# Whole tiles first in both expert layers, four row buffers in the first, and no closing drain of GpSimd

## The chip, the cores and the metric

The kernel runs on one core of one Trainium2 chip. The metric is the time of one execution on the device in microseconds (us); lower is better. One execution was also taken by the hardware profiler, and the rows below come from that one.

## The reference, cut to what matters

Two layers, each of a conditioning block and an expert block with two experts per token, on 2048 tokens of 512 numbers:

```python
x = x + L0_ffn(L0_cond(x))      # attention over a paged cache, then 8 sparse weight sets, 2 per token
x = x + L1_ffn(L1_cond(x))      # linear with a low-rank adapter, then 8 experts, 2 per token
# L0_ffn: logits = clip(xt @ gate_w.T); top 2, softmax; per expert a sparse delta added to W
# L1_ffn: probs = softmax(x @ gate_w); top 2
h = gelu(x @ fc1_w[e] + fc1_b[e], approximate=False)
y = h @ fc2_w[e] + fc2_b[e];    out = sum over the 2 chosen e of combine[t, e] * y
```

With 2 experts per token, 4096 rows go through each expert layer. The router's choices are known only while the kernel runs. Worked out from the reference with its inputs, the eight experts get 542, 416, 510, 556, 504, 526, 508 and 534 rows in the first layer and 542, 526, 490, 492, 520, 543, 510 and 473 in the second.

## The kernel before, in words

**Routing.** Every token's row (512 numbers and four of bookkeeping, `DX` = 516) is sent by GpSimd with an indirect DMA (`send`) to each of its two experts' regions in a DRAM tensor, `rows`. The semaphores `xs_sc` (first layer) and `x2_sc` (second) count these sends. VectorE keeps a running end of each region (`run`); when the last token is placed, `ends()` signals `r_end`, and `tiles()` makes the list of tiles: for tile t of 39 (`NTILE`) the expert (`ex_i`) and the first row (`row_i`) of 128 rows, in order of experts, each expert's partly filled tile right behind its full ones. It signals `r_ok`. 39 is the most that 4096 rows in 8 regions can need; tiles past the last used one read a region of zeros.

**Zeros.** Because a partly filled tile reads past its region's end, 128 rows of zeros are written behind each of the eight ends (`zero_ends`: for each expert a register load of the end and a DMA of 258 KB), four by the SP queue and four by the ACT queue, as soon as `r_end` is there. The semaphore `zrows` counts them. SP waits for `zrows` and for all sends before it fetches the first tile.

**First expert layer.** Tiles go in pairs through two slots. SP fetches the rows into `xs_in[s]` (two buffers); the next fetch into a buffer waits until TensorE has turned it (`l_tx`) and VectorE has copied the four bookkeeping columns (`l_mt`, in `take_meta`). TensorE turns four 128x128 blocks, ScalarE copies them to `xs_t`, TensorE multiplies with the expert's weights (`m_w`), VectorE scales out of PSUM into `y_sb[s]` (line 1801), and GpSimd adds the rows to `acc0` or `acc1` in DRAM by an indirect DMA (line 653). VectorE may write `y_sb[s]` again only when that DMA has landed (`l_st`). Behind each of the first eight pairs ScalarE issues a load of 1 MB of the second layer's weights (`load_fc`). Before the first tile TensorE also waits for `m_done` = 16, the signal of VectorE's last addition to the weights (line 1556), which stands in VectorE's order behind `tiles()`.

**Second expert layer.** The same with `xs_in[s]`, but VectorE copies the turned rows (`turned1`, line 1867), ScalarE copies the expert's fc1 matrix (`weights`, line 1211) and does the gelu, and the rows are added to `out`. A pair is 80 matmuls or so on TensorE.

**The end.** The five engines' programs stand in a block. At its end each engine drains (line 66), and all of them meet. GpSimd comes there last, after it has waited for the last addition into `out`.

Of the kernel before, what the change touches and what calls it, by code (L numbers as in the profile page):

```python
# [9 lines left out]
I32 = mybir.dt.int32  # L10
# [4 lines left out]
P = 128  # L15
# [21 lines left out]
PAIRS = (NTILE + 1) // 2  # L37
BOTH, LAST = (0, 1), tuple(range(NTILE - 2 * (PAIRS - 1)))
# [25 lines left out]
def program(nc, d):  # L64
    ctx = ExitStack()
    with ctx:
# [33 lines left out]
        tile_ii = words(R3, 7700, [NTILE], I32)  # L100
# [37 lines left out]
        xs_in = [words(R3, DX * s, [DX]) for s in range(2)]  # L138
        xs_t = [words(R3, 1032 + 512 * s, [KC, P]) for s in range(2)]
        h_t = [words(R3, 2056 + 512 * s, [KC, P]) for s in range(2)]  # L140
        y_sb = [words(R3, 3080 + 512 * s, [D]) for s in range(2)]
        fc1_s = [words(R3, 4104 + 2048 * s, [KC, D]) for s in range(2)]
# [102 lines left out]
        ntf = [sb(f"ntf{i}", [P, NE]) for i in range(4)]  # L245
        slot_f = sb("slot_f", [P, 2, 2])
        slot_i = sb("slot_i", [P, 2, NT], I32)
        ex_c = words(masks, 0, [NTILE, NE])
        ex_f = sb("ex_f", [P, NTILE])
# [3 lines left out]
        tile_io = sb("tile_io", [P, NTILE])  # L253
# [15 lines left out]
        for name in ("rope_d gain_d p0_dma table_d imp_d mask_d atoms_d w_kv w_q raw_dma consts zero_ok rope_in rope_r idx_ok idx_n eaw_in imp_s eaw_ok mark_in mark_ok "  # L269
                     "delta wgt_ok eqa cell_ok pre_w pre_c b1_p zdone r_end zrows mscat bk bc e_in e_lg e_row "  # L270
                     "s_dot s_mx s_exp s_sc s_pt s_pe s_pv s_ot m_done att_w kv_mm kv_sq kv_nr rst step p1r p1o o_p1 o_k o_kc q_ss q_nw q_rp xq "
                     "r_sel r_slot r_ok l_f l_ex l_mt k_mt r_l r_lexp acc_z xs_sc x2_sc w5 w1_ok b1_d b2_d fc1_d fc2_d c_rt c_rtc").split():
            S[name] = sem(name)
        S2 = {}
        for name in ("mstage kvd kvc "
                     "l_in l_tx l_xt l_mm l_ye l_st k_in k_tx k_xt k_w k_m1 k_hg k_m2 k_ye k_yb k_st "
                     "c_in c_x1 c_tx c_xt c_xa c_xe c_h c_x2 c_g c_st").split():
            S2[name] = sem2(name)
        S4 = {name: [sem(f"{name}_{i}") for i in range(4)] for name in ("x_in", "p1k")}
# [26 lines left out]
        block = ctx.enter_context(nc.Block())  # L306
# [10 lines left out]
        def _(sp):  # L317
# [104 lines left out]
            def expert_io(layer, sent, load, read, meta_read):  # L422

                def fetch(row, s):
                    sp.dma_start(xs_in[s], rows_d[bass.ds(row, P), :]).then_inc(load[s], 16)

                def rows_of(t, slots=BOTH):
                    return [sp.value_load(row_i[0:1, bass.ds(t + s, 1)], min_val=0, max_val=ROWS - P) for s in slots]

                def following(i, slots):  # L430
                    rows = rows_of(2 * i + 2, slots)
                    sp.wait_ge(meta_read, i + 1)
                    for s in slots:
                        sp.wait_ge(read[s], i + 1)
                        fetch(rows[s], s)

                sp.wait_ge(S["r_ok"], layer)
                rows = rows_of(0)
                sp.wait_ge(S["zrows"], 16 * NE * layer)
                sp.wait_ge(sent, 32 * NT)  # L440
                for s in range(2):
                    fetch(rows[s], s)
                yield
                with sp.Fori(0, PAIRS - 2) as i:
                    following(i, BOTH)
                following(PAIRS - 2, LAST)
# [31 lines left out]
            io = expert_io(2, S["x2_sc"], S2["k_in"], S2["k_tx"], S["k_mt"])  # L478
            next(io)
            sp.dma_start(b2_bc, d["b2"].partition_broadcast(P)).then_inc(S["b2_d"], 16)  # L480
            for _ in io:
                pass
# [3 lines left out]
        def _(po):  # L486
            po.iota(iot[:, 0:32], [[1, 32]], base=0, channel_multiplier=0)
            po.iota(iot[:, 32:33], [[0, 1]], base=0, channel_multiplier=1)
            po.iota(tile_ii, [[1, NTILE]], base=0, channel_multiplier=0)
# [188 lines left out]
        def _(pe):  # L678
# [205 lines left out]
            def turn_x(load, done, turned, i, s):  # L884
                pe.wait_ge(load[s], 16 * i + 16)
                wait(pe, done[s], i)
                turn4(ps[:, s, :], xs_in[s]).then_inc(turned[s], 1)

            def layer0(i, now, after):
                es = [pe.value_load(ex_i[0:1, bass.ds(2 * i + s, 1)], min_val=0, max_val=NE - 1) for s in now]  # L890
                for s in now:
                    pe.wait_ge(S2["l_xt"][s], i + 1)
                    wait(pe, S2["l_ye"][s], i)
                    chunks(ps[:, 2 + s, :], lambda k: xs_t[s][:, k, :], lambda k: m_w[:, k, es[s], :]
                           ).then_inc(S2["l_mm"][s], 1)
                    if s in after:
                        turn_x(S2["l_in"], S2["l_xt"], S2["l_tx"], i + 1, s)

            for s in range(2):
                turn_x(S2["l_in"], S2["l_xt"], S2["l_tx"], 0, s)  # L900
            with pe.Fori(0, PAIRS - 2) as i:
                layer0(i, BOTH, BOTH)
            layer0(PAIRS - 2, BOTH, LAST)
            layer0(PAIRS - 1, LAST, ())

# [51 lines left out]
            def layer1(i, now, after):  # L957
# [9 lines left out]
                for s in after:  # L967
                    turn_x(S2["k_in"], S2["k_xt"], S2["k_tx"], i + 1, s)
# [6 lines left out]
            for s in range(2):  # L975
                turn_x(S2["k_in"], S2["k_xt"], S2["k_tx"], 0, s)
            with pe.Fori(0, PAIRS - 2) as i:
                layer1(i, BOTH, BOTH)
# [5 lines left out]
        def _(ac):  # L984
# [143 lines left out]
            zero_ends(ac, 1, range(NE // 2, NE))  # L1128
# [69 lines left out]
            zero_ends(ac, 2, range(NE // 2, NE))  # L1198
# [26 lines left out]
            with ac.Fori(0, PAIRS - 2) as i:  # L1225
                gelu(i, BOTH, BOTH)
# [5 lines left out]
        def _(ve):  # L1232
# [410 lines left out]
            def tiles():  # L1643

                def step(ins):
                    ve.drain()
                    return ins
                ve.drain()
                step(TT(ntf[0][:], run[:], region0[:], ALU.subtract))
                step(TS(ntf[0][:], ntf[0][:], float(P - 1), None, ALU.add))  # L1650
                step(CP(nti[:], ntf[0][:]))
                step(TS(nti[:], nti[:], 7, None, ALU.arith_shift_right))
                CP(ntf[2][:], nti[:])
                step(CP(ntf[0][:], nti[:]))
                u, v = ntf[0], ntf[1]
                for sh in (1, 2, 4):
                    TT(v[:, sh:], u[:, sh:], u[:, :NE - sh], ALU.add)
                    step(CP(v[:, :sh], u[:, :sh]))
                    u, v = v, u
                TS(ntf[3][:], ntf[2][:], -float(P), float(REGION), ALU.mult, ALU.add)  # L1660
                ve.drain()
                step(TT(ex_c[:], u[:].unsqueeze(1).broadcast_to([P, NTILE, NE]),
                        tile_io[:].unsqueeze(2).broadcast_to([P, NTILE, NE]), ALU.is_le))
                step(red(ex_f[:], ex_c[:, :, 0:NE - 1], ALU.add))
                CP(ex_i[:], ex_f[:])
                TS(ex_r[:, 0:NTILE], ex_f[:], -1.0, float(NE), ALU.mult, ALU.add)
                step(TT(ex_c[:], ex_c[:], ntf[3][:].unsqueeze(1).broadcast_to([P, NTILE, NE]), ALU.mult))
                step(red(ex_f[:], ex_c[:], ALU.add))
                step(ve.scalar_tensor_tensor(ex_f[:], tile_io[:], float(P), ex_f[:], ALU.mult, ALU.add))
                CP(row_i[:], ex_f[:])  # L1670
                ve.drain().then_inc(S["r_ok"], 1)
                CP(run[:], region0[:])
# [91 lines left out]
            tiles()  # L1764
# [4 lines left out]
            def take_meta(i, load, slots, taken):  # L1769

                for s in slots:
                    ve.wait_ge(load[s], 16 * i + 16)
                    CP(meta[:, s, :], xs_in[s][:, D:DX])
                ve.drain().then_inc(taken, 1)

# [7 lines left out]
            def layer0(i, slots, after):  # L1783
# [4 lines left out]
                if after:  # L1788
                    take_meta(i + 1, S2["l_in"], after, S["l_mt"])
# [13 lines left out]
            take_meta(0, S2["l_in"], BOTH, S["l_mt"])  # L1803
            mark(x2_rows, 0, NT)
            with ve.Fori(0, PAIRS - 2) as i:
                layer0(i, BOTH, BOTH)
            layer0(PAIRS - 2, BOTH, LAST)
            layer0(PAIRS - 1, LAST, ())
# [50 lines left out]
            tiles()  # L1859
            for s in range(2):  # L1860
                ve.wait_ge(S2["c_st"][s], 16 * (NT // 2))
# [7 lines left out]
            def layer1(i, now, after):  # L1869
# [9 lines left out]
                if after:  # L1879
                    take_meta(i + 1, S2["k_in"], after, S["k_mt"])  # L1880
# [12 lines left out]
            take_meta(0, S2["k_in"], BOTH, S["k_mt"])  # L1893
# [66 lines left out]
```

## Time and profile before

| | |
|---|---|
| time, median of 3 runs | 1059.96 us (1058.91, 1059.96, 1066.42) |
| time of the profiled execution | 1056.38 us |
| its span, first to last instruction | 1054.2 us |
| mean granted clock of TensorE | 0.952 |

The span is what the rows below divide up. The profiled execution took 2.2 us more than its span; that rest lies outside of all instructions shown. The profiled execution was 3.6 us (0.34%) below the median.

### The profile page before, as it was taken

The page shows a single profiled execution, that of the slowest core. Times are in us where ns is not written, and L with a number is a line of the kernel's source. Part 1 is how long each engine was busy: PE and PEld are TensorE (multiplying, and loading weights), DVE is VectorE, ACT ScalarE, POOL GpSimd, SP SyncE. Part 2 cuts the span into 40 slices and gives each one's busy share as a digit, 9 for nine tenths or more (in the row PEclk, how much of TensorE's full clock was granted, in tenths as well). Part 3 has the DMA queues.
Part 4 walks back from the last instruction along what each step waited for, and adds up shares of the span by engine and source line. Part 5 has one row for each costly group of instructions (what it writes and reads, how often), then busy time and mean ns, then how long its engine had stood idle before and what let it go on. Part 6 is the DMA issues. An engine that isn't in the chain of part 4 may idle for free.

```text
span 1054.2 us, 18329 instructions
## 1 busy us (share of the span) xinstructions
PE 932.6 (88%) x4690; PEld 604.2 (57%) x4691; DVE 547.0 (52%) x2190; ACT 416.5 (40%) x1273; POOL 364.7 (35%) x475
## 2 busy tenths in 40 slices
PE   6999998989998888379899969994799999999994
PEld 2457555555455444234344438884577777777772
DVE  4777687776678987623334424555233333333331
ACT  3654465555655555011111112221354455444540
POOL 3575244666663250313334321324022121222121
PEclk9996999999999999779999989998799999999998
DMA  7854923353355361578777747974442334323430
GB/s 249 271 221 138 343 63 102 82 146 94 72 162 163 105 222 60 183 234 218 204 161 137 131 110 244 387 278 167 175 80 46 68 68 78 60 61 66 77 47 0
DMA packets 76455, 152.11 MB, mean 144 GB/s; under 512 B 16743, under 2 KB 22007, under 8 KB 74736
## 3 DMA queue, kind: packets, MB, share of 16 engines
q1 hardware_dynamic: 40240, 87.27, 25.0%
q0 software_dynamic: 24832, 42.71, 20.1%
q10 hardware_dynamic: 11328, 21.51, 6.2%
q8 instruction: 20, 0.33, 0.1%
q14 instruction: 35, 0.29, 0.1%
HBM read 94.05 MB, written 69.00 MB: 155 GB/s over the span
## 4 chain that ended last, share of the span: by engine, by line
PE 63%; DVE 13%; DMA 9%; issue 7%; ACT 2%; DVEq 2%; SPq 1%; POOL 1%; ACTq 0%; POOLq 0%
PE ps L681 52%; DMA acc<-R,tok_i 5%; PE ps L687 4%; DVE R L1538 2%; PE ps L751 2%; DVE R L1556 2%; DVE R L1527 2%; ACT R L1042 1%; PE ps L739 1%; DMA R<-rows 1%; DMA rows<-zrow 1%; DMA R<-m_buf 1%; PE ps L732 1%; DMA R<-in_x_t 1%; PE ps L783 1%
## 5 line engine op out<-in xcount | busy, mean ns | idle before, releaser
L681 PE MATMUL ps<-R 128*128 128x128 f32 (+4 forms) x2768 | 685.3, 404 | 15.7 <-DMA R<-in_x_t 10.4
L681 PEld LDWEIGHTS ps<-R 128*128 128x128 f32 x2768 | 420.4, 194 | 240.2 <-issue 217.6
L653 POOL DMA_INDIRECT out_x<-R,tok_i x39 | 60.5, 1552 | 249.0 <-DVEq L1892 160.8
L687 PE MATMUL ps<-ident,R 128*128 128x128 f32 x440 | 67.6, 286 | 55.3 <-DMA R<-rows 39.0
L580 POOL DMA_INDIRECT rows<-R,slot_i x64 | 65.7, 1026 | 137.1 <-ACT lg L1174 73.2
L1058 ACT ACTIVATE R<-R,nmx 128x384 f32<-128x384 f32 x128 | 78.4, 622 | 77.7 <-DVE nmx L1527 77.7
L687 PEld LDWEIGHTS ps<-ident,R 128*128 128x128 f32 x440 | 53.8, 147 | 89.1 <-issue 75.8
L653 POOL DMA_INDIRECT acc<-R,tok_i x39 | 60.5, 1552 | 117.1 <-DVE R L1801 107.5
L1527 DVE CUSTOM_DVE_ANT_0 R<-ps,R,q_scale 128x384 f32<-128x384 f32 x128 | 73.7, 613 | 30.5 <-issue 30.5
L1219 ACT ACT_TABLE_LOAD x18 | 23.1, 1283 | 145.5 <-PE ps L681 145.5
L739 PE MATMUL ps<-ident,R 128*128 128x128 f32 x384 | 56.5, 283 | 24.5 <-DVE R L1538 13.0
L1887 DVE TENSOR_TENSOR R<-ps,R 128x512 f32<-128x512 f32 x39 | 27.0, 692 | 95.9 <-PE ps L681 95.9
L1211 ACT ACTIVATE R<-R 128x2048 f32 x39 | 75.6, 1940 | 1.4 <-issue 1.4
L739 PEld LDWEIGHTS ps<-ident,R 128*128 128x128 f32 x384 | 42.8, 143 | 49.8 <-DVE R L1538 25.5
L588 POOL DMA_INDIRECT m_buf<-tot,cell_i x32 | 51.4, 1607 | 37.1 <-DMA m_buf<-tot,cell_i 29.8
L1144 ACT ACTIVATE R<-ps 128x512 f32<-128x512 f32 x39 | 23.3, 597 | 95.1 <-PE ps L687 93.1
L732 PE MATMUL ps<-R 64*128 64x384 f32 x256 | 60.0, 548 | 0.9 <-ACT R L1031 0.9
L1064 ACT ACTIVATE R<-ps 128x384 f32<-128x384 f32 x128 | 56.7, 508 | 6.2 <-PE ps L739 6.1
L1867 DVE COPY R<-ps 128x512 f32<-128x512 f32 x39 | 25.3, 687 | 53.3 <-PE ps L687 53.1
L1219 ACT ACTIVATE R<-ps,inv_f 128x128 f32<-128x128 f32 x156 | 44.8, 381 | 18.4 <-PE ps L681 18.2
L1538 DVE TENSOR_SCALAR R<-R,rsum 128x384 f32<-128x384 f32 x128 | 49.2, 427 | 5.0
L751 PE MATMUL ps<-R 128*64 128x256 f32 x384 | 49.3, 392 | 0.0
(282 smaller groups left out, 919.2 us busy)
## 6 DMA issues: line engine op xcount, KB each, us to landing
R<-rows SPq DMA_DIRECT2D x78, 258.0 KB, 3.4
R<-in_fc ACTq DMA_DIRECT2D x16, 1024.0 KB, 6.6
m_buf<-R SPq DMA_DIRECT2D x8, 1024.0 KB, 8.2
R<-m_buf SPq DMA_DIRECT2D x16, 512.0 KB, 4.7
R<-acc SPq DMA_DIRECT2D x32, 256.0 KB, 5.9
R<-in_x_t SPq DMA_DIRECT2D x4, 1024.0 KB, 8.8
R<-in_x_t SPq DMA_DIRECT2D x8, 512.0 KB, 3.4
new_kv<-R SPq DMA_DIRECT2D x16, 256.0 KB, 3.1
```

The costliest lines, as they stand in the source:

```text
L580: po.indirect_dma_start(out=rows_d, out_offset=bass.IndirectOffsetOnAxis(ap=slot_i[:, c, t:t + 1], axis=0), in_=rows[:, t, :], in_offset=N ...
L653: po.indirect_dma_start(out=sums[s], out_offset=bass.IndirectOffsetOnAxis(ap=tok_i[:, s:s + 1], axis=0), in_=y_sb[s], in_offset=None, boun ...
L681: m = pe.matmul(out, lhs(k), rhs(k), start=(k == 0 and first), stop=(k == KC - 1 and last))
L687: m = pe.transpose(out[:, k * P:(k + 1) * P], src[:, k * P:(k + 1) * P], ident[:])
L732: pe.matmul(ps[:, 2 + u % 4, 0:KW], q_t[s][base:base + 64, jj, qt * P:(qt + 1) * P], k_t[s][base:base + 64, p, qt * P:qt * P + KW], start= ...
L739: m = pe.transpose(ps[:, 6 + u % 2, c * P:(c + 1) * P], prob[u % 4][:, c * P:(c + 1) * P], ident[:])
L751: n = pe.matmul(ps[HD * x:HD * (x + 1), 1, KC // 2 * P * (m % 2):KC // 2 * P * (m % 2 + 1)].rearrange("p (i q) -> p i q", q=P), kv[s][:, q ...
L1058: ac.activation(prob[u % 4], msk_s[u % 4], ACT.Exp, bias=nmx[:, u:u + 1], scale=-1.0, accum_out=sums[:, u:u + 1]).then_inc(S["s_exp"], 1)
L1211: ac.activation(fc1_s[s], fc1[:, :, e, :], ACT.Copy).then_inc(S2["k_w"][s], 1)
L1219: g = ac.activation(h_t[s][:, c, :], ps[:, 2 + s, c * P:(c + 1) * P], ACT.Gelu, bias=b1_t[:, e, c:c + 1])
L1527: ve.tensor_tensor_reduce(out=msk_s[u % 4], in0=ps[:, 2 + u % 4, 0:KW], in1=mask[:, u // NH, :], scale=q_scale[:, B % 2, u:u + 1], scalar= ...
L1538: TS(prob[u % 4], prob[u % 4], rsum[:, u % NH:u % NH + 1], None, ALU.mult).then_inc(S["s_sc"], 1)
```

## The change

Seven things are changed.

1. `tiles()` makes the list in two parts. The first 24 tiles (`FULL`) are taken from those whose 128 rows are all taken; 24 of them there are always. It signals `r_ok` behind these. Then it works out the other 15 (`REST`): the whole tiles that are left, then the partly filled ones, then unused ones. Behind these it signals a new semaphore, `q_ok`. In the first layer VectorE's last addition to the weights stands behind both parts.
2. SP fetches the first tiles on `r_ok` and the sends alone, and waits for `zrows` and `q_ok` only before it fetches the tile with index 24. TensorE, and in the second layer ScalarE, wait for `q_ok` at the same place in their loops, which are cut in two there.
3. SP's four writes of zeros follow its first fetches (in the second layer also the load of `b2_bc`, 2 MB).
4. ScalarE's four writes of zeros move: in the first layer behind the second pair's `load_fc`; in the second behind the first two copies of fc1 and a new wait for `x2_sc`.
5. The first layer's rows have four buffers. Four tiles are fetched at the start, and the pair i+2 is fetched when the pair i is turned and its bookkeeping is copied. Its loops do two pairs per turn.
6. Some buffers of `R3` shift by 8 words to make room.
7. The block is opened with `no_gpsimd_drain=True`.

```diff
-        block = ctx.enter_context(nc.Block())
+        block = ctx.enter_context(nc.Block(no_gpsimd_drain=True))
...
+            sp.wait_ge(S["r_ok"], 1)
+            rows = rows_of(0, range(4))
+            sp.wait_ge(S["xs_sc"], 32 * NT)
+            for b in range(4):
+                fetch(rows[b], b, S4["l_in"][b])
             zero_ends(sp, 1, range(NE // 2))
-            for _ in expert_io(1, S["xs_sc"], S2["l_in"], S2["l_tx"], S["l_mt"]):
-                pass
+            with sp.Fori(0, FP // 2 - 1) as h:
+                rows0(2 * h, 0)
+                rows0(2 * h + 1, 2)
+            sp.wait_ge(S["q_ok"], 1)
+            sp.wait_ge(S["zrows"], 16 * NE)
+            with sp.Fori(FP // 2 - 1, PAIRS // 2 - 2) as h:
+                rows0(2 * h, 0)
+                rows0(2 * h + 1, 2)
...
+            sp.wait_ge(S["r_ok"], 2)
+            rows = rows_of(0)
+            sp.wait_ge(S["x2_sc"], 32 * NT)
+            for s in BOTH:
+                fetch(rows[s], s, S2["k_in"][s])
+            sp.dma_start(b2_bc, d["b2"].partition_broadcast(P)).then_inc(S["b2_d"], 16)
             zero_ends(sp, 2, range(NE // 2))
...
-            zero_ends(ac, 1, range(NE // 2, NE))
             ac.wait_ge(S["xs_sc"], 32 * NT)
...
                 load_fc(fc1, fc1_v, i, S["fc1_d"])
+                if i == 1:
+                    zero_ends(ac, 1, range(NE // 2, NE))
...
-            zero_ends(ac, 2, range(NE // 2, NE))
...
             for s in range(2):
                 weights(0, s)
-            with ac.Fori(0, PAIRS - 2) as i:
+            ac.wait_ge(S["x2_sc"], 32 * NT)
+            zero_ends(ac, 2, range(NE // 2, NE))
+            with ac.Fori(0, FP - 1) as i:
+                gelu(i, BOTH, BOTH)
+            ac.wait_ge(S["q_ok"], 2)
+            with ac.Fori(FP - 1, PAIRS - 2) as i:
                 gelu(i, BOTH, BOTH)
```

The second part of the new `tiles(layer)`, in full:

```python
ve.drain().then_inc(S["r_ok"], 1)
CP(seg_end[:, 0:NE], u[:])
step(ve.scalar_tensor_tensor(n_row, n_full, -float(P), n_row, ALU.mult, ALU.add))
step(TS(n_part, n_row, 0.0, None, ALU.is_gt))
u = ends_of(n_part, ntf[0], ntf[1])          # three steps of two instructions
TS(seg_end[:, NE:2 * NE], u[:], seg_end[:, NE - 1:NE], None, ALU.add)
step(ve.scalar_tensor_tensor(n_gap, n_part, -float(P), ntf[3][:], ALU.mult, ALU.add))
CP(seg_gap[:, 0:NE - 1], ntf[3][:, 0:NE - 1])
step(ve.scalar_tensor_tensor(seg_gap[:, NE - 1:NE], n_full[:, 0:1], float(P), ntf[3][:, NE - 1:NE], ALU.mult, ALU.add))
TS(seg_gap[:, NE - 1:NE], seg_gap[:, NE - 1:NE], -float(NE * REGION), None, ALU.add)
ve.scalar_tensor_tensor(seg_gap[:, NE:2 * NE - 1], n_full[:, 1:NE], float(P), n_gap[:, 0:NE - 1], ALU.mult, ALU.add)
CP(seg_gap[:, 2 * NE - 1:2 * NE], n_gap[:, NE - 1:NE])
step(ve.memset(seg_e, 1.0))
ve.memset(seg_e[:, NE - 1:NE], 1.0 - NE)
step(ve.memset(seg_e[:, 2 * NE - 1:2 * NE], 0.0))
...
shape = [P, REST, 2 * NE]
step(TT(c, seg_end.unsqueeze(1).broadcast_to(shape), tile_io[:].unsqueeze(2).broadcast_to(shape), ALU.is_le))
step(TT(w, c, seg_e.unsqueeze(1).broadcast_to(shape), ALU.mult))
step(red(ex_f[:, 0:REST], w, ALU.add))
CP(ex_i[:, FULL:], ex_f[:, 0:REST])
TS(ex_r[:, FULL:NTILE], ex_f[:, 0:REST], -1.0, float(NE), ALU.mult, ALU.add)
step(TT(w, c, seg_gap.unsqueeze(1).broadcast_to(shape), ALU.mult))
step(red(ex_f[:, 0:REST], w, ALU.add))
step(ve.scalar_tensor_tensor(ex_f[:, 0:REST], tile_io[:], float(P), ex_f[:, 0:REST], ALU.mult, ALU.add))
CP(row_i[:, FULL:], ex_f[:, 0:REST])
ve.drain().then_inc(S["q_ok"], 1)
```

## Rows read from the trace of the kernel before

**Rows 1.** The page, its chain that ended last, shares by line.

```profile
PE ps L681 52%; DMA acc<-R,tok_i 5%; PE ps L687 4%; DVE R L1538 2%; PE ps L751 2%; DVE R L1556 2%; DVE R L1527 2%; ACT R L1042 1%; PE ps L739 1%; DMA R<-rows 1%; DMA rows<-zrow 1%; DMA R<-m_buf 1%; PE ps L732 1%; DMA R<-in_x_t 1%; PE ps L783 1%
```

**Rows 2.** Stretches: us, busy PE, PEld, DVE, ACT, POOL, clock, DMA share, GB/s.

```profile
463.00:620.00 157.00, 148.87 (x450) 71.35 (x448) 62.49 (x264) 26.00 (x56) 58.99 (x38) 1.00 0.73 165
...
757.00:1041.00 284.00, 282.58 (x1645) 207.47 (x1643) 92.67 (x319) 128.92 (x206) 58.96 (x38) 1.00 0.34 62
```

**Rows 3.** The last addition: the chain, its landing, and line 66's drain.

```profile
1043.46 1.55 POOL out_x L653
```

```profile
out_x<-R,tok_i POOLq DMA_INDIRECT x1, 2.7
```

```profile
L66 POOLq DRAIN  x1: 7579/7579/7579, 1046.4 to 1046.4; - x1
```

**Rows 4.** The chain into the first expert layer: start, length, what.

```profile
444.81 5.55 DMA rows<-zrow
450.52 2.66 DMA R<-rows
453.32 1.94 PE ps L687 x8
```

**Rows 5.** The chain into the second expert layer.

```profile
741.87 2.54 DMA R<-rows
...
746.49 0.89 issue
747.38 9.71 PE ps L681 x64
```

**Rows 6.** SP's wait for the sends, when it ended in each layer.

```profile
L440 SPq EVENT_SEMAPHORE  x2: 17/17/17, 449.0 to 740.8; - x2
```

**Rows 7.** GpSimd's last sends of both layers, in order of time.

```profile
443.00 0.96 POOL L580 DMA_INDIRECT rows<-R,slot_i  x1 [0.30 <-issue]
...
734.54 0.96 POOL L580 DMA_INDIRECT rows<-R,slot_i  x1 [0.30 <-issue]
```

**Rows 8.** Landing of two sends: that of 728.16 us, that of 734.54 us.

```profile
DMA to landing us min/median/max: 2.7/2.7/2.7
...
DMA to landing us min/median/max: 6.2/6.2/6.2
```

**Rows 9.** VectorE in the old list, in order of time.

```profile
441.79 0.17 DVE L1660 TENSOR_SCALAR ntf<-ntf 128x8 f32<-128x8 f32 x1
442.03 0.48 DVE L1662 TENSOR_TENSOR masks<-ntf,tile_io 128x312 f32<-128x312 f32 x1
```

**Rows 10.** VectorE around the end of the list, in order of time.

```profile
445.05 1.07 DVE L1556 TENSOR_TENSOR R<-R 128x512 f32<-128x512 f32 x1
...
735.56 0.18 DVE L1670 CAST row_i<-ex_f 128x39 int32<-128x39 f32 x1
```

**Rows 11.** SP's register loads of tile rows: count, min/median/max ns.

```profile
L428 SPq TENSOR_LOAD <-row_i x78: 261/268/1024, 445.2 to 997.0; - x78
```

**Rows 12.** ScalarE's queue, its four writes of zeros.

```profile
440.21 4.78 ACTq L313 DMA_DIRECT2D rows<-zrow  x4
```

**Rows 13.** The chain in the first expert layer: two of the additions.

```profile
469.19 7.17 DMA acc<-R,tok_i
...
505.86 8.01 DMA acc<-R,tok_i
```

**Rows 14.** Waits in 466 to 536 us: total, times, longest.

```profile
PE ps L687 <- DMA R<-rows: 5.5, 5, 1.3
...
PE ps L681 <- DVE R L1801: 1.0, 5, 0.2
```

**Rows 15.** Stretches as in group 2.

```profile
466.00:476.00 10.00, 10.00 (x34) 5.04 (x33) 2.99 (x13) 2.00 (x4) 3.17 (x3) 1.00 0.92 216
...
744.00:746.00 2.00, 1.46 (x7) 1.34 (x8) 0.68 (x3) 0.00 (x0) 0.00 (x0) 0.50 1.11 386
...
752.00:754.00 2.00, 2.00 (x18) 2.00 (x18) 0.34 (x2) 0.38 (x1) 0.00 (x0) 0.94 0.05 18
```

More of the change, by code:

```diff
@@ L420, in _ @@
                 fetch_m(m)
[L422 to L446, printed above, removed]
@@ L448, in _, with rows_of, fetch, rows0 @@
-            zero_ends(sp, 1, range(NE // 2))
-            for _ in expert_io(1, S["xs_sc"], S2["l_in"], S2["l_tx"], S["l_mt"]):
-                pass
+            def rows_of(t, slots=BOTH):
+                return [sp.value_load(row_i[0:1, bass.ds(t + s, 1)], min_val=0, max_val=ROWS - P) for s in slots]
+            def fetch(row, b, load):
+                sp.dma_start(xs_in[b], rows_d[bass.ds(row, P), :]).then_inc(load, 16)
+            def rows0(i, b, slots=BOTH):
+                rows = rows_of(2 * i + 4, slots)
+                sp.wait_ge(S["l_mt"], i + 1)
+                for s in slots:
+                    sp.wait_ge(S2["l_tx"][s], i + 1)
+                    fetch(rows[s], b + s, S4["l_in"][b + s])
@@ L476, in _ @@
                 sp.wait_ge(S2["c_tx"][s], NT // 2)
-            zero_ends(sp, 2, range(NE // 2))
[L478 to L482, printed above, removed]
+            sp.wait_ge(S["r_ok"], 2)
+            rows = rows_of(0)
+            sp.wait_ge(S["x2_sc"], 32 * NT)
+            for s in BOTH:
+                fetch(rows[s], s, S2["k_in"][s])
+            sp.dma_start(b2_bc, d["b2"].partition_broadcast(P)).then_inc(S["b2_d"], 16)
+            zero_ends(sp, 2, range(NE // 2))
+            with sp.Fori(0, FP - 1) as i:
+                rows1(i)
+            sp.wait_ge(S["q_ok"], 2)
+            sp.wait_ge(S["zrows"], 32 * NE)
+            with sp.Fori(FP - 1, PAIRS - 2) as i:
+                rows1(i)
+            rows1(PAIRS - 2, LAST)
         @block.gpsimd
@@ L882, in _, with turn_x, turn_x0, turn_x2 @@
             pe.wait_ge(S["m_done"], 16)
-            def turn_x(load, done, turned, i, s):
-                pe.wait_ge(load[s], 16 * i + 16)
+            def turn_x(x, load, landed, done, turned, i, s):
+                pe.wait_ge(load, landed)
                 wait(pe, done[s], i)
-                turn4(ps[:, s, :], xs_in[s]).then_inc(turned[s], 1)
-            def layer0(i, now, after):
+                turn4(ps[:, s, :], x).then_inc(turned[s], 1)
+            def turn_x0(i, h, b, s):
+                turn_x(xs_in[b + s], S4["l_in"][b + s], 16 * h + 16, S2["l_xt"], S2["l_tx"], i, s)
+            def turn_x2(i, s):
+                turn_x(xs_in[s], S2["k_in"][s], 16 * i + 16, S2["k_xt"], S2["k_tx"], i, s)
+            def layer0(h, odd, now, after):
+                i = 2 * h + odd
                 es = [pe.value_load(ex_i[0:1, bass.ds(2 * i + s, 1)], min_val=0, max_val=NE - 1) for s in now]
@@ L967, in layer1 @@
                 for s in after:
[L968 removed]
+                    turn_x2(i + 1, s)
                 for s in now:
@@ L975, in _ @@
             for s in range(2):
-                turn_x(S2["k_in"], S2["k_xt"], S2["k_tx"], 0, s)
-            with pe.Fori(0, PAIRS - 2) as i:
+                turn_x2(0, s)
+            with pe.Fori(0, FP) as i:
+                layer1(i, BOTH, BOTH)
+            pe.wait_ge(S["q_ok"], 2)
+            with pe.Fori(FP, PAIRS - 2) as i:
                 layer1(i, BOTH, BOTH)
@@ L1641, in ends, with tiles @@
                 ve.drain().then_inc(S["r_end"], 1)
-            def tiles():
+            def tiles(layer):
                 def step(ins):
@@ L1652, in tiles @@
+                step(CP(nti[:], n_row))
                 step(TS(nti[:], nti[:], 7, None, ALU.arith_shift_right))
[L1653 to L1660, printed above, removed]
@@ new lines, in tiles @@
+                if layer == 1:
+                    for s in range(2):
+                        ve.wait_ge(S2["c_st"][s], 16 * (NT // 2))
+                c, w = rest_c[layer], rest_m[layer]
+                shape = [P, REST, 2 * NE]
+                step(TT(c, seg_end.unsqueeze(1).broadcast_to(shape), tile_io[:].unsqueeze(2).broadcast_to(shape), ALU.is_le))
+                step(TT(w, c, seg_e.unsqueeze(1).broadcast_to(shape), ALU.mult))
+                step(red(ex_f[:, 0:REST], w, ALU.add))
@@ L1763, in _ @@
             ends()
-            tiles()
+            tiles(0)
             for _ in adds:
@@ L1858, in _ @@
             ends()
-            tiles()
-            for s in range(2):
-                ve.wait_ge(S2["c_st"][s], 16 * (NT // 2))
+            tiles(1)
             def turned1(i, slots):
@@ L1879, in layer1 @@
                 if after:
-                    take_meta(i + 1, S2["k_in"], after, S["k_mt"])
+                    meta1(i + 1, after)
                 if after:
```

112 lines of the change are left out of this document (73 added, 39 removed).

## The prediction

> **What bounds the kernel now.** I read the chain that ended last first. TensorE's matmuls carry half of it [rows 1]; the writes of zeros, the fetches of rows and the additions into `acc` carry 1%, 1% and 5%. The stretches say where TensorE is not full: in the second expert layer it is busy for 282.6 of 284 us, in the first for 148.9 of 157 [rows 2]. So a change to the order of tiles can win at four places only: at the end, at the two entries and in the 8.1 us of gaps inside the first layer.
>
> At the end the last addition is issued at 1043.46 and lands 2.7 us later, at 1046.2 [rows 3]. Then GpSimd drains for 7.58 us, and the kernel ends with it.
>
> At both entries the chain runs through a write of zeros: it lands at 450.36, SP fetches at 450.52, the rows land 2.66 us later, TensorE starts at 453.32 [rows 4]. In the second layer the fetch is at 741.87 and the first matmul of fc1 at 747.38 [rows 5]. The zeros cost twice. They are waited for, and they make the sends slow: a send shortly before them lands in 2.7 us, the last one, in their midst, in 6.2 [rows 8], so that SP has all sends only at 449.0 and 740.8 [rows 6].
>
> Inside the first layer, the chain is one of additions of slot 1: each lands 7.2 to 8.0 us after its issue [rows 13], each beside a load of 1 MB. The five waits of TensorE for rows (5.5 us) are followed by five short waits for VectorE's scaling (1.0 us) [rows 14]. Both end together: VectorE could scale only when the addition before had landed.
>
> **The closing drain.** One instruction of 7.58 us goes [rows 3]; nothing else is at work then, and what is late next is the meeting of the engines at 1046.4 plus some 0.2 us. Ends: 0 (the time comes again elsewhere) and 7.6. I take **-7.6**, since GpSimd's own wait has already seen the last landing, and nothing that is computed hangs on the drain.
>
> **Entry to the second layer.** The sends: the last is issued at 734.54 [rows 7]; without zeros beside it it lands in 2.7 us [rows 8], at 737.25. The list: the old one was ready at 735.75 [rows 10]. Its new first part has one small step and one small copy less (0.24 + 0.08 us), and four large instructions shrink from 312 elements or so to 192. By the slope of the two rows [rows 9], (0.48 - 0.17) / 304 = 1.02 ns an element, that is 4 x 0.12. It is ready 0.8 us earlier, at 734.95. Two register loads of 0.27 to 1.0 us [rows 11], each with some 0.3 us of checks behind it (an estimate), are done by 737.5. The fetch goes at about 737.4 in place of 741.87, the rows land at 739.95 and are turned by 742.05; with 0.89 us of TensorE's own loads [rows 5] fc1 could start at 742.95.
>
> VectorE must by then have copied the turned rows, and it has got the second part of the list. Small steps stand 0.24 us apart [rows 9]: 11 of them (first scalar-tensor step, comparison, three of `ends_of`, two gaps, two memsets, the row number, the last cast) are 2.6 us; 5 large steps of 240 elements, 0.41 + 0.07 each, 2.4; a dozen instructions without a drain between, about 0.08 each, 1.0. Sum 6.0 us, to 741.0. Then bookkeeping and the first copy: about 742.3. That is 0.65 us ahead of TensorE, so it is hidden, just. **-4.4 us** (747.38 to 742.95). Ends: -2.2, if the clock (below) or a long second part takes half; -4.6.
>
> ScalarE's zeros now stand behind its first fc1 copies; its queue needs 4.8 us for them [rows 12], from about 740.2 to 745, and the first gelu is due only when the first tile's fc1 is through, after 748. SP's zeros stand ahead of the second pair's fetch, as they stood ahead of the first; that fetch leaves at about 745.5 and has until TensorE has done 64 matmuls, 9.7 us [rows 5], at 752.6. With the 2 MB of `b2_bc`, 4.6 MB are moved in the 15 us between: 310 GB/s, less than the 386 that 744 to 746 us reach [rows 15]. I cost both at 0; without that cover it would be up to 2 us.
>
> **Entry to the first layer.** The last send is issued at 443.00 [rows 7], lands at 445.7. SP has four register loads now, so it fetches between 446.4 and 449 and has rows at 449.1 to 451.7. But TensorE also waits for VectorE's last addition to the weights. It was at 445.05 and took 1.07 us [rows 10], under cover of the zeros. Now the second part stands ahead: 444.2 + 6.0 + 0.1 + 1.1 = 451.4. That cover is gone, and the addition becomes the gate: TensorE starts at 451.5 in place of 453.32, **-1.8 us**. Ends: -3 (rows as gate), 0 (a longer second part).
>
> **Inside the first layer.** Four buffers take away the five waits for rows. Yet the matmul behind each waits for VectorE's scaling, and that for a landed addition; only the 0.2 us each by which the scaling was waited for after the turn come free, and only the last stays won: **-0.2 us**. End: -8.1, all gaps of group 2.
>
> ScalarE's four zeros, 1.03 MB, now follow its second load on the same queue. They meet the addition of 469.19, which landed in 7.17 us [rows 13] at a DMA share of 0.92 [rows 15], and the next one. If these two become like the later ones (8.0), the chain of slot 1 grows by 0.8 twice: **+1.6 us**. Ends: 0, if the zeros fall in a gap; +2.7, if all of the 1.03 MB, at 386 GB/s [rows 15], is put in front. The 4.8 us for which ScalarE issues them [rows 12] end about when its next copy is due; the additions' chain covers a delay of some 3 us. Here page and row can be weighed. The trace shows the additions slow beside one long load and not stopped by it. The Trainium skill (DMA: Bandwidth & Descriptors, Queues, rings and completion order) says that each DMA engine takes turns between the queues that have work. By that rule zeros queued behind a load on the same queue don't take a larger share from the additions, only for a longer time, which would bring the sum nearer to +0.8 than to +2.7.
>
> The order itself: the counts give 28 whole tiles, 8 partly filled and 3 unused in both layers. Slot 0 loses two nearly empty tiles (30 and 32 rows) early; slot 1's first eight were whole before. 0. `q_ok` comes more than 50 us ahead of its use: its waits, and what is queued behind them, cost 0. Buffers that shift: 0.
>
> **The clock** is a cost that no edit names. TensorE comes cold from its wait for the rows: granted 0.50 (1.2 GHz) at 744 to 746, and 0.94 in the mean of 752 to 754 [rows 15], so it rose to 1.00 (2.4 GHz) at about 752.2. If it rises as long after the start as now, the starts won are kept whole. If it rises at the old instant, half of them is given back: 0.9 + 2.2 us.
>
> **Sum**: -7.6 - 4.4 - 1.8 - 0.2 + 1.6 = **-12.4 us**, so 1044.0 in place of the profiled 1056.4, or 1.17% less. The median stands 0.34% above the profiled execution. On the median's scale: 1059.96 x 0.9883 = **1047.5 us**.
>
> **Rivals.**
> (a) *The drain's time isn't won.* For it: 2.2 us of the time lie outside the span already, and something at the program's end may wait for what the drain waited for. Against it: the last DMA has landed. -4.8 us, 1055.1. The Trainium skill (Runtime: NRT & Kernel Launch, The ~15µs preamble/postamble breakdown) tells of a barrier and a reset of the DMA rings after the kernel; if that had to wait for GpSimd, it would be this case. No row here shows it.
> (b) *Starts half given back*, by the clock, or by VectorE's second part being 2 us longer than worked out: -12.4 + 3.1 = -9.3, 1050.7.
> (c) *Four buffers free the additions.* If it is the late fetches that make additions and fetches collide, all gaps go: -12.4 + 0.2 - 8.1 = -20.3, 1039.6. Against it: an addition's chain has no term in which rows are waited for.
> (d) *Slower.* The additions of slot 1 collide longer at each of the seven links from 469 to 534 us, because the start shifts against the loads and more is queued. To eat up 12.4 us takes 1.8 us a link, 9.8 in place of 8.0; from there it decides. At 2.5 us a link it is +5, 1065. Against it: the loads are issued by the same loop, in step with the additions, so the phase hardly moves.
> (e) *The change doesn't do what it says*: fetches still wait late, on the sends. Were they as slow without the zeros, both entries would win next to nothing: -7.6, 1052.4. The 2.7 us of the send in calm speaks against it.
>
> **How the numbers follow.** Forecast 0.65 (1044.5 to 1050.5, with the bounds of the entries and the zeros); (a) 0.10; (b) 0.13; (c) 0.04; (d) 0.03; (e) 0.05. A change of 1%, 10.6 us, is about what this kernel's runs can tell from none, and the limit is 1049.4. Of the forecast 0.88 lies below it: 0.57; with (c) and a third of (b), faster is 0.66. Slower is (d) alone, 0.03; the rest, 0.31, lies within 1%. The range takes in (b), (e) and (a), down to the forecast's lower bound less what medians of this kernel scatter: 1042 to 1055.5.
>
> **What would show it.** No long drain behind the last landing. Last sends landing in about 3 us in both layers. The first turn near 451.5, behind the last addition to the weights, not behind rows; fc1's first matmul near 743. In the first layer no waits for rows, but gaps of the same total, now all on VectorE's scaling. The addition beside ScalarE's zeros at about 8 us. The forecast is wrong if the drain's time turns up elsewhere, if VectorE's second part takes 8 us or more, or if those gaps are gone.

## The result, and the profile after

The changed kernel takes 1045.58 us (median of 4 runs, 1044.44 to 1049.75). The kernel before, timed again beside it, takes 1061.52 us (4 runs). The ratio is 0.9874, with a 95% interval of 0.9837 to 0.9912: 1.26% faster, where 1.17% was forecast. The span of the profiled execution went from 1054.2 to 1044.2 us.

The two traces are best laid beside each other in seven stretches, cut at instructions that both kernels have: the cast of `end_i` (the region ends are known), TensorE's first turn of the first expert layer, the issue of that layer's last addition, the cast of `end_i` in the second layer, the first matmul of fc1, the issue of the last addition, and the end. Each length is the difference of two starts in the trace of that kernel, good to about 0.05 us (us):

| stretch | before | after | difference | forecast |
|---|---|---|---|---|
| A start to first end cast | 439.10 | 437.20 | -1.9 | 0 |
| B to the first turn | 14.22 | 12.19 | -2.0 | -1.8 |
| C to the first layer's last addition | 166.69 | 168.06 | +1.4 | +1.4 |
| D to the second end cast | 109.99 | 111.75 | +1.8 | 0 |
| E to the first matmul of fc1 | 17.38 | 14.21 | -3.2 | -4.4 |
| F to the last addition | 296.08 | 297.71 | +1.6 | 0 |
| G to the end | 10.74 | 3.08 | -7.7 | -7.6 |

**The end.** The first lines are from the chain that ended last, the next ones from the instructions of line 68, where the engines meet (line 66 before). The drain of [rows 3] is missing: GpSimd comes to its branch at 1043.9 and no drain follows. What is left behind the last addition is its issue and landing.

```profile
1041.12 1.55 POOL out_x L676
```

```profile
L68 PEldq DRAIN  x1: 3338/3338/3338, 1035.4 to 1035.4; - x1
L68 DVEq DRAIN  x1: 19/19/19, 1040.3 to 1040.3; - x1
L68 POOLq COMPARE_BRANCH  x1: 46/46/46, 1043.9 to 1043.9; - x1
```

**Entry to the first layer**, in order of time. It answers to [rows 4, 10]: SP fetches 7.8 us after the end cast, but TensorE waits for the addition to the weights (line 1600), which stands behind the second part of the list. The bracket names it.

```profile
445.00 1.93 SPq L432 DMA_DIRECT2D R<-rows  x4
447.69 3.66 SPq L319 DMA_DIRECT2D rows<-zrow  x4
...
448.22 1.06 DVE L1600 TENSOR_TENSOR R<-R 128x512 f32<-128x512 f32 x1
...
449.39 1.94 PE L710 MATMUL ps<-ident,R 128*128 128x128 f32 x8 [14.58 <-DVE R L1600]
```

The last sends are calm now, in both layers, against 6.2 us in [rows 8]; this is the landing of the second layer's last send, of 733.62 us (the first layer's, of 441.11, has the same 2.7):

```profile
DMA to landing us min/median/max: 2.7/2.7/2.7
```

**Entry to the second layer**, in order of time; it answers to [rows 5].

```profile
736.54 0.89 SPq L432 DMA_DIRECT2D R<-rows  x2
...
737.07 4.02 ACTq L319 DMA_DIRECT2D rows<-zrow  x4
...
737.47 0.43 SPq L497 DMA_DIRECT2D R<-in_b  x1
...
739.25 3.65 SPq L319 DMA_DIRECT2D rows<-zrow  x4
...
741.54 1.11 PE L710 MATMUL ps<-ident,R 128*128 128x128 f32 x4 [0.94 <-DMA R<-rows]
...
743.41 9.82 PE L704 MATMUL ps<-R 128*128 128x128 f32 x64 [0.76 <-issue]
```

SP fetches at 736.54, 7.3 us behind the end cast, where it was 11.9 (741.87 in [rows 5]): 4.5 us sooner, as forecast. Then ScalarE's zeros, `b2_bc` and SP's zeros are all issued within 6 us, and slot 1's rows of the first pair are late: the turn at 741.54 waits for them. The next pair is worse. The fetches issued between 745 and 746 us landed 9.3 us later (last number: us to landing). In the kernel before, the fetches at this place had only the 2 MB of `b2_bc` ahead of them and took 6.8 us. The two lines are after and before:

```profile
R<-rows SPq DMA_DIRECT2D x2, 258.0 KB, 9.3
...
R<-rows SPq DMA_DIRECT2D x2, 258.0 KB, 6.8
```

TensorE waited once more, at 754.31; in the kernel before it didn't wait here:

```profile
754.31 1.31 PE L710 MATMUL ps<-ident,R 128*128 128x128 f32 x8 [1.07 <-DMA R<-rows]
```

In 736 to 756 us the issues by kind (medians) show what was in the way: zeros that took over 10 us to land, against 4.5 to 4.7 us in the kernel before, where they were issued right behind the end cast.

```profile
R<-in_b SPq DMA_DIRECT2D x1, 2048.0 KB, 9.9
R<-rows SPq DMA_DIRECT2D x6, 258.0 KB, 3.6
rows<-zrow ACTq DMA_DIRECT2D x4, 258.0 KB, 10.6
rows<-zrow SPq DMA_DIRECT2D x4, 258.0 KB, 10.9
```

**Inside the first layer.** First the chain's additions of slot 1, which answer to [rows 13]; then ScalarE's zeros, in order of time; then the waits of 462 to 536 us, which answer to [rows 14].

```profile
463.65 10.07 DMA acc<-R,tok_i
...
475.40 8.09 DMA acc<-R,tok_i
...
485.16 7.56 DMA acc<-R,tok_i
```

```profile
464.04 4.95 ACTq L319 DMA_DIRECT2D rows<-zrow  x4
```

```profile
PE ps L704 <- DVE R L1886: 9.0, 7, 1.8
...
PE ps L704 <- ACT R L1182: 0.5, 1, 0.5
```

The waits for rows are gone, and in their place stand waits for VectorE's scaling: 9.0 us in seven, and 0.5 for ScalarE, where all waits together were 6.5 us in ten. The zeros start 0.4 us after the addition of 463.65, which took 10.1 us.

### The profile page after: what moved, and what is told of

The parts are those of the page before. It is cut to its first block, busy times and chain, and to the rows that moved or that the text cites. A ratio compares the mean times of both kernels' runs of the same rounds, so it can differ in the third digit from the quotient of the medians.

```text
span 1044.2 us, 18359 instructions
## 1 busy us (share of the span) xinstructions
PE 928.9 (89%) x4690; PEld 602.9 (58%) x4691; DVE 553.5 (53%) x2242; ACT 407.9 (39%) x1266; POOL 365.9 (35%) x475
## 4 chain that ended last, share of the span: by engine, by line
PE 63%; DVE 14%; DMA 9%; issue 7%; ACT 3%; DVEq 2%; POOL 1%; SPq 1%; POOLq 0%; ACTq 0%
PE ps L704 52%; DMA acc<-R,tok_i 6%; PE ps L710 4%; DVE R L1582 2%; PE ps L774 2%; DVE R L1600 2%; DVE R L1571 2%; ACT R L1081 1%; PE ps L762 1%; DMA R<-m_buf 1%; PE ps L755 1%; DMA R<-rows 1%; DMA R<-in_x_t 1%; PE ps L806 1%; PE ps L797 1%
```

## The experiments

The seven stretches of all runs, cut as above (us). E and F belong together, as B and C do, since what starts early may wait later.

| run | A | B | C | D | E | F | G | span |
|---|---|---|---|---|---|---|---|---|
| before | 439.1 | 14.22 | 166.69 | 109.99 | 17.38 | 296.08 | 10.74 | 1054.2 |
| after | 437.2 | 12.19 | 168.06 | 111.75 | 14.21 | 297.71 | 3.08 | 1044.2 |
| 1 before, no drain | 442.8 | 14.24 | 167.57 | 112.29 | 17.39 | 295.79 | 3.12 | 1053.2 |
| 2 after, with drain | 443.8 | 12.17 | 168.26 | 110.57 | 14.41 | 297.21 | 10.68 | 1057.1 |
| 3 layer 2's zeros late | 443.1 | 12.20 | 167.93 | 110.87 | 12.65 | 294.91 | 3.14 | 1044.8 |
| 4 ScalarE's zeros after the loads | 443.0 | 12.24 | 169.37 | 109.69 | 14.65 | 296.74 | 3.11 | 1048.8 |
| 5 two-buffer timing | 443.9 | 12.18 | 168.34 | 109.88 | 14.29 | 298.19 | 3.12 | 1049.9 |
| 6 addition to the weights first | 443.5 | 10.81 | 169.97 | 110.22 | 14.52 | 297.66 | 3.12 | 1049.8 |
| 7 fc1 loads spread | 444.4 | 12.27 | 164.11 | 111.32 | 13.65 | 299.92 | 3.13 | 1048.8 |
| 8 ScalarE's zeros on SP, late | 444.1 | 12.21 | 166.27 | 110.52 | 14.35 | 298.65 | 3.10 | 1049.2 |
| 9 runs 3, 7 and 8 together | 442.3 | 12.27 | 160.88 | 110.95 | 12.56 | 296.54 | 3.10 | 1038.6 |

Stretch A runs the same instructions as in the kernel before but for the length of one iota, and it varies by 7 us; run 1 is the kernel before up to its end, and is 3.7 us longer there. So a comparison by single spans misleads here, and the runs are read by the stretches B to G. D varies by 2.6 us in the same way. Runs 3, 4, 5, 6 and 8 were timed once each, so what they show is read from their traces alone; runs 1, 2, 7 and 9 have ratios from several timings.

The stretches still hold one thing that no edit sets: how soon TensorE's clock rises behind the start of each layer. How long the same first matmuls took shows it (us). The last column is TensorE's wait for the rows of the second layer's second pair.

| run | first tile of the first layer | first 64 matmuls of fc1 | wait for the second pair's rows |
|---|---|---|---|
| before | 6.69 | 9.71 | none |
| after | 5.10 | 9.82 | 1.07 |
| 1 | 6.30 | 9.42 | none |
| 2 | 5.74 | 9.06 | 1.35 |
| 3 | 5.71 | 8.37 | none |
| 4 | 5.71 | 8.81 | 1.13 |
| 5 | 5.41 | 9.21 | 2.18 |
| 6 | 6.04 | 8.91 | 1.95 |
| 7 | 5.87 | 8.06 | 3.61 |
| 8 | 6.28 | 9.04 | 2.81 |
| 9 | 5.78 | 10.17 | none |

So differences of C under about 1.5 us, and of E and F under about 2, can be the clock's. E and F together are 313.5 and 313.2 us in the kernel before and run 1, and 311.4 to 313.6 us in the seven kernels that keep the changed order of the second layer.

**Run 1: the kernel before without the drain.**

```diff
-        block = ctx.enter_context(nc.Block())
+        block = ctx.enter_context(nc.Block(no_gpsimd_drain=True))
```

> The kernel before with only the closing drain of GpSimd taken away. My theory (the drain's 7.58 us lie inside the time and come again nowhere): 7.6 us, 0.72%, faster than the kernel before; in the trace less than 1 us between the last landing and the end. Rival (the time comes again elsewhere): within 2 us of the kernel before.

Measured in 9 runs against 19: ratio 0.9922 (0.9895 to 0.9949), 0.78% or 8.3 us. G is 3.12 us in place of 10.74. The drain's time was in the measured time, and the trace shows it nowhere else.

**Run 2: the changed kernel with the drain.**

```diff
-        block = ctx.enter_context(nc.Block(no_gpsimd_drain=True))
+        block = ctx.enter_context(nc.Block())
```

> The changed kernel with the closing drain put back. My theory: some 4 to 5 us (0.4 to 0.5%) faster than the kernel before, span near 1051.8, with a drain of 7.6 us behind the last landing. Rival (a drain is long because of what was done late, so the new order would shorten it): a drain of under 4 us and a span near 1047.

Ratio 0.9951 (0.9931 to 0.9971) in 11 runs against 19, 0.49% or 5.2 us (3.1 to 7.3): this is the worth of all the rest of the change. Stretches B, C, E and F, which the change touches, show less: 2.3 us against the kernel before and 2.9 against run 1. Where the rest lies is not shown. The drain is as long as it was, to the nanosecond (instructions of line 68):

```profile
L68 POOLq DRAIN  x1: 7579/7579/7579, 1049.3 to 1049.3; - x1
```

So its length doesn't depend on the order of tiles, and the rival falls. The two ratios multiplied give 0.9873, the ratio of the whole change: the parts add up. The span expected, 1051.8, was missed, by stretch A.

**Run 3: the second layer's zeros behind the fetches.**

```diff
-            sp.dma_start(b2_bc, d["b2"].partition_broadcast(P)).then_inc(S["b2_d"], 16)
-            zero_ends(sp, 2, range(NE // 2))
-            with sp.Fori(0, FP - 1) as i:
+            rows1(0)
+            sp.dma_start(b2_bc, d["b2"].partition_broadcast(P)).then_inc(S["b2_d"], 16)
+            rows1(1)
+            zero_ends(sp, 2, range(NE // 2))
+            with sp.Fori(2, FP - 1) as i:
                 rows1(i)
...
+            gelu(0, BOTH, BOTH)
             ac.wait_ge(S["x2_sc"], 32 * NT)
             zero_ends(ac, 2, range(NE // 2, NE))
-            with ac.Fori(0, FP - 1) as i:
+            with ac.Fori(1, FP - 1) as i:
```

> The changed kernel with the second layer's zeros and the load of b2_bc behind the next fetches: SP fetches pair 1 first, then loads b2_bc, fetches pair 2, then writes its zeros; ScalarE writes its zeros after the first pair's gelu. Theory (zeros and b2_bc queued ahead delay the rows of pairs 0 and 1): slot 1's rows of pair 0 and the rows of pair 1 land within 4 us, TensorE doesn't wait at 753, and from the end cast to the last addition's issue it is 1.5 to 2.5 us shorter than in the changed kernel (311.96). Rival (the rows are late for want of DMA bandwidth, whatever the order): the same 312 within 0.5.

E and F together are 307.56 us in place of 311.92: 4.4 us shorter, where 1.5 to 2.5 were expected. In part that is the clock, which rose sooner here: the 64 matmuls of fc1 took 8.37 us, 1.5 less than in the changed kernel. That leaves some 3 us for the order (an estimate from the two traces). In order of time, TensorE turns both slots at once and doesn't wait for the second pair:

```profile
744.32 1.94 PE L712 MATMUL ps<-ident,R 128*128 128x128 f32 x8 [13.03 <-DMA R<-rows]
746.75 8.37 PE L706 MATMUL ps<-R 128*128 128x128 f32 x64 [0.50 <-issue]
754.96 1.04 PE L712 MATMUL ps<-ident,R 128*128 128x128 f32 x8
```

Its four fetches of the first two pairs landed in 2.6 to 3.8 us. The same bytes are moved in both kernels; only what stands in front in the queues differs. Run 9 has the same order and a slow clock (10.17 us for the 64 matmuls), and still E and F are 309.10:

```profile
738.96 10.17 PE L707 MATMUL ps<-R 128*128 128x128 f32 x64 [0.54 <-DVE R L1954]
```

All seven kernels that keep the changed order wait for the second pair's rows, for 1.1 to 3.6 us, and runs 3 and 9 don't. That the order costs is shown; how much of it is SP's own queue and how much ScalarE's zeros was not separated.

**Run 4: ScalarE's zeros of the first layer behind the eighth load.**

```diff
-                if i == 1:
+                if i == 2 * KC - 1:
                     zero_ends(ac, 1, range(NE // 2, NE))
```

> The changed kernel with ScalarE's zeros of the first layer behind its eighth load instead of its second. Theory (they cost by colliding with the first additions and by holding ScalarE): the addition issued near 463.6 lands in 7 to 8 us in place of 10.1, the stretch from the first turn to the last addition's issue in the first layer (168.06 us) gets 2 to 3 us shorter; some of it may come back at the new place, where the loads end. Rival (the chain of additions only shifts): the same within 0.7 us.

Half right. The first addition of slot 1 landed in 6.9 us, and the seventh was issued 82.5 us after the end cast, 3.1 us sooner than in the changed kernel (85.6). But C is 1.3 us longer, 0.6 of it in the first tile (5.71 us in place of 5.10). In order of time, ScalarE's zeros and what followed:

```profile
526.81 5.05 ACTq L319 DMA_DIRECT2D rows<-zrow  x4
...
532.10 1.09 ACT L1182 ACTIVATE R<-ps 128x512 f32<-128x512 f32 x2 [6.41 <-issue]
532.83 5.39 PE L704 MATMUL ps<-R 128*128 x8 [3.79 <-ACT R L1182]
```

ScalarE issues for 5 us and copies nothing; TensorE waits 3.8 us for the copy. Here no slow addition hides this. The wait cost more than its own length: right behind it the granted clock fell, to a mean of 0.57 over 533 to 537 us, and the tile's eight matmuls took 5.4 us, against 3.7 for the eight before.

```profile
533.00:537.00 4.00, 4.00 (x6) 1.67 (x7) 1.93 (x10) 0.39 (x2) 1.29 (x1) 0.57 1.07 318
```

The zeros thus have two costs: the collision, and the hold of the engine that issues them. The collision isn't always as large: the addition of 525.50, which has a load and these zeros beside it, landed in 8.5 us.

**Run 5: the timing of two buffers.**

```diff
-                sp.wait_ge(S["l_mt"], i + 1)
+                sp.wait_ge(S["l_mt"], i + 2)
                 for s in slots:
-                    sp.wait_ge(S2["l_tx"][s], i + 1)
+                    sp.wait_ge(S2["l_tx"][s], i + 2)
```

> The changed kernel, but a fetch in the first layer waits until the pair before it, not the one before that, is turned: the timing of two buffers after the first four tiles. My theory (the chain of additions sets the pace, four buffers win only the last 0.2 us): five to seven waits of TensorE for rows are back, yet the stretch from the first turn to the last addition's issue stays at 168.1 within 0.7 us. Rival (four buffers free the additions): 3 to 8 us longer.

The waits for rows are back (total, times, longest, from 28 us behind the end cast to the last addition), and C is 168.34 in place of 168.06 us:

```profile
PE ps L704 <- DVE R L1886: 4.0, 7, 1.1
...
PE ps L710 <- DMA R<-rows: 3.9, 4, 1.3
```

The difference of 0.3 us is what the first tile took longer here by the clock (5.41 in place of 5.10), so no gain by the four buffers is shown. Waits changed their name; the chain of additions sets the pace.

**Run 6: the addition to the weights ahead of the second part.**

```diff
-            def tiles(layer):
+            def tiles(layer, between=()):
...
                 ve.drain().then_inc(S["r_ok"], 1)
+                for _ in between:
+                    pass
...
-            tiles(0)
-            for _ in adds:
-                pass
+            tiles(0, adds)
```

> The changed kernel with VectorE's last addition to the weights between the two parts of the list, in the first layer. My theory (the second part of 6 us ahead of it gates the start): TensorE then waits for the rows; the first turn follows the end cast by 10.3 to 11.2 us in place of 12.2. Rival (the rows land no earlier than that): 12.0 or more.

B is 10.81 us, and the wait ends by the rows:

```profile
454.31 1.94 PE L710 MATMUL ps<-ident,R 128*128 128x128 f32 x8 [13.17 <-DMA R<-rows]
```

So the gate was the second part of the list, as worked out. But C grew by 1.9 us: the first addition of slot 1 was issued 26.3 us after the end cast (26.5 in the changed kernel) and again took 10.1 us. The first tile's matmuls took 6.04 us, against 5.10, and they were done 19.9 us behind the end cast, against 20.0: the start was won at half clock and lost there. B and C together are 0.5 us longer, which the traces can't tell from nothing.

**Run 7: fc1 in 16 pieces over 16 pairs.**

```diff
-            for i in range(2 * KC):
+            for i in range(4 * KC):
                 layer0(i)
-                load_fc(fc1, fc1_v, i, S["fc1_d"])
+                k, e = i // 4, slice(NE // 4 * (i % 4), NE // 4 * (i % 4 + 1))
+                ac.dma_start(fc1[:, k, e], fc1_v[:, k, e]).then_inc(S["fc1_d"], 16)
...
-            with ac.Fori(2 * KC, PAIRS - 1) as i:
+            with ac.Fori(4 * KC, PAIRS - 1) as i:
```

with the two waits on `fc1_d` raised to 64 * KC.

> The changed kernel with the 8 MB of fc1 loaded in 16 pieces of 0.5 MB over 16 pairs, in place of 8 of 1 MB over 8. Theory (additions are slow because each runs beside a load of 1 MB, and that makes the gaps of the first layer): additions of slot 1 land in 6 to 7 us, the gaps of TensorE mostly go, the stretch from the first turn to the last addition's issue gets 5 to 9 us shorter (near 161), 0.5 to 0.8% faster than the changed kernel. Rival (an addition is slow by itself or beside the row fetches): additions of slot 1 stay near 8 us and twice as many pairs are slow, 5 us or more longer.

C is 164.11 us, 4.0 us shorter (4.7 if the first tile had taken as long as in the changed kernel), short of the 5 to 9 expected. The theory held: behind the one beside ScalarE's zeros (9.2 us), the additions of slot 1 in the chain landed in 6.1 to 6.7 us, and the rival falls. The waits for the scaling, over the whole stretch, fell from 9.0 us to

```profile
PE ps L704 <- DVE R L1887: 3.1, 6, 1.0
```

Against the kernel before the ratio is 0.9838 (0.9796 to 0.9881) in 4 runs against 7, not told apart from that of the changed kernel. One reason stands in the trace of the second layer, whose code is the changed kernel's: TensorE was soon through its first matmuls, then waited 3.6 us for the second pair's rows, and E and F are 313.57 us, 1.6 more.

```profile
757.43 1.97 PE L710 MATMUL ps<-ident,R 128*128 128x128 f32 x8 [3.61 <-DMA R<-rows]
```

**Run 8: ScalarE's zeros of the first layer on SP, behind the fetch of the 24th tile.**

```diff
-                if i == 1:
-                    zero_ends(ac, 1, range(NE // 2, NE))
...
+            zero_ends(sp, 1, range(NE // 2, NE))
             sp.wait_ge(S["q_ok"], 1)
             sp.wait_ge(S["zrows"], 16 * NE)
```

> The changed kernel with ScalarE's four zeros of the first layer given to SP, behind the fetch of the 24th tile, where no load is left and nobody waits on SP for 15 us. Theory (two costs: the collision with the first additions, 3 us, and the hold of ScalarE, which cost 5.7 us at the place behind the eighth load): both go; no gap behind the eighth load, and the stretch from the first turn to the last addition's issue is 164 to 166 us (168.06 in the changed kernel, 169.37 with the zeros behind the eighth load). Rival (the gap of 5.7 us was the end of the loads' own backlog): it stays, and the stretch is 168 or more.

C is 166.27 us: 1.8 us less than the changed kernel and 3.1 us less than run 4, just above the range given; the clock took 1.2 us of it (6.28 for the first tile). The first addition of slot 1 landed in 7.3 us. The gap of run 4 is gone, so it was the hold.

**Run 9: runs 3, 7 and 8 together.**

> The changed kernel with all three: the second layer's zeros and b2_bc behind the fetches, ScalarE's zeros of the first layer on SP behind the 24th tile, and the fc1 loads in 16 halves. Theory (the three costs are separate): first layer's stretch 159 to 162 us in place of 168.06, second layer from the end cast to the last addition's issue 307.5 in place of 311.9; in all 10 to 13 us, 1.0 to 1.2% faster than the changed kernel, a ratio to the kernel before of 0.975 to 0.978. Rival (the gains overlap, since a freed chain meets the next limit): 0.981 or more.

The ratio to the kernel before is 0.9771 (0.9736 to 0.9806) in 6 runs against 10, median 1040.75 us: about 1.0% faster than the changed kernel, by the two ratios. C is 160.88, 7.2 us shorter; runs 7 and 8 alone gave 4.0 and 1.8. Set to the changed kernel's first tile, the three are 7.9, 4.7 and 3.0: the two gains add up, and neither helps or hinders the other beyond that. E and F are 309.10, 1.5 us more than in run 3; the 64 matmuls took 1.8 us longer. This version beats both kernels.

## Why the prediction was right

**The closing drain**: -7.6 forecast, -7.7 in the trace, 8.3 us by run 1's ratio (5.4 to 11.2). Rival (a) is out.

**Entry to the first layer**: -1.8 forecast, -2.0 measured. The steps held as well: the sends landed in 2.7 us, the second part of the list lasted from 442.2 to 448.1 (6.0 forecast), and the addition to the weights was the gate. Run 6 shows it.

**Inside the first layer**: +1.4 forecast, +1.4 measured, but that is luck: TensorE's waits grew by 3.0 us (6.5 to 9.5), and the clock gave 1.6 back. Four buffers were put at 0.2 us and show nothing beyond the clock (run 5); rival (c) is out. The collision with the zeros was sized at 0.8 us for each of two additions; the first took 10.1 in place of 7.2 us and the next of slot 1 8.1 in place of 7.0. I had taken 8.0 as a ceiling from the later additions, and it is none; the addition of slot 0 between the two took 8.9 us, in place of 5.8, and had no term. The rule weighed there (the Trainium skill, DMA: Bandwidth & Descriptors, Queues, rings and completion order: each DMA engine takes turns between queues) had pointed to a small cost; this trace has +2.9 us for the one addition, and run 4, with those zeros moved away, has 6.9 us for it. So the measurement goes against the small cost that I drew from the rule; the rule itself no run here tests. Against that stands the clock, which rose sooner behind the start: the first tile's matmuls took 5.1 us, against 6.7 before.

```profile
451.00:456.00 5.00, 4.21 (x8) 1.83 (x7) 1.00 (x7) 0.99 (x4) 0.00 (x0) 0.60 0.84 245
...
453.00:463.00 10.00, 8.87 (x20) 4.65 (x21) 2.58 (x17) 1.52 (x4) 0.00 (x0) 0.54 0.73 247
```

The first line, of the changed kernel, has a mean clock of 0.60; with levels of 0.50 and 1.00 the rise is at 455, 5.6 us behind the first turn. The second, of the kernel before, has 0.54, so the rise is at about 462, 9 us behind the first turn. So the clock did not give back half, as in rival (b), but added some 1.6 us of luck.

**Entry to the second layer**: the term that was mis-sized is the cover of the second pair's fetch, which I took as 0, "up to 2 us". E won 3.2 us, not 4.4, mostly since slot 1's rows were late (0.9 us); VectorE was in time, as worked out, since fc1's first matmul waited for TensorE's own issue alone; F lost 1.6, of which 1.1 is the wait for the second pair's rows. Of 4.4 us only 1.5 were won in this pair of traces, 2.9 less than forecast, and by all seven kernels with this order about 1.0. Run 3 gets 5.9 us (313.46 to 307.56), but 1.3 of these are the clock (8.37 us for the 64 matmuls, 9.71 before). Run 9, where they took 10.17, gets 4.4, so the 4.4 us forecast are there once the fetches go ahead. My error was to compare bytes with bandwidth, 4.6 MB in 15 us. The transfers did fit; but a fetch issued last behind 3 MB on its queue landed in 9.3 us, behind 2 MB in 6.8 and with neither ahead in 2.6 to 3.8. The clock rose 5.1 us behind the first matmul here, about as before, when it was 4.9 (748 to 749 us, mean 0.73):

```profile
748.00:749.00 1.00, 1.00 (x9) 1.00 (x8) 0.00 (x0) 0.00 (x0) 0.00 (x0) 0.73 1.27 248
```

**The sum** promised 2.4 us more than the span gave (-12.4 forecast, -10.0 measured). The second layer's fetches fell short by 2.9; A and D, which had no term, cancel. The difference of medians was -15.9 us, more than either; the runs of both kernels scatter by several us, as stretches A and D show, so that the agreement of 1.26% with 1.17% is partly chance. By runs 1 and 2 the drain makes up 0.78% and the rest 0.49%.

## What to carry to other kernels

A wait that is taken away is worth only what the queue then does with it: work moved from ahead of a first fetch to behind it stands ahead of the second, and bytes that fit the bandwidth can still make the one small transfer late that somebody waits for. Issue what is needed first, then the rest, on a queue whose engine has nothing else to do. Before two traces are compared to the microsecond, see how long the same first matmuls took in each: here the clock moved a stretch by up to 1.8 us, and one and the same order (runs 3 and 9) differs by 1.5. When a wait changes its name from one releaser to another and the stretch keeps its length, look for the chain behind both, here one buffer that comes free when an addition has landed.

## What the runs showed of the hardware

The closing drain of GpSimd takes 7.58 us with nothing left in flight (no DMA packet in the trace from 1046.5 us on), in both kernels whose trace has it, and nothing at the end takes its place when it is left out. Four writes of 258 KB hold the issuing ScalarE for 4.0 to 5.1 us; where nothing covered it, TensorE waited 3.8 us and then ran for 3.4 at half clock. An indirect addition that lands in 4.7 to 5.9 us in calm took 6.9 to 8.3 in slot 1, beside a load of 1 MB, 6.1 to 6.7 beside loads of 0.5 MB, and 8.5 to 10.1 beside a load and four writes. A fetch of 258 KB landed in 2.5 to 3.8 us with nothing large ahead of it on its queue, in 6.8 behind 2 MB and in 9.3 behind 3 MB with ScalarE's writes beside it. The granted clock of TensorE rose between 5.6 and about 9 us behind the first turn of the first expert layer, in kernels that differ little there, so that an earlier start can be worth more or less than its own length.
